# A conditioned sequence network on one core: the state-space layers' sums, D term and input projection placed at other units, and the output rows of layer 3 gathered one batch later

## The reference

```python
xn = layernorm(x) * (1 + scale) + shift          # layer 3: then xn = xn[:, perm]
x_in, z = split(xn @ W_in)                       # 512 channels each
u = silu(conv1d(x_in, 4 taps) + conv_b)
dt_r, B, C = split(u @ W_xproj)                  # 64, 16 and 16 columns
dt = softplus(dt_r @ W_dt + b_dt)
for t in range(512):                             # lax.scan over the tokens
    h = h * exp(dt[t] * A) + (dt[t] * u[t]) * B[t]    # 512 channels x 16 states
    y[t] = sum over the states of h * C[t]
y = (y + u * D) * silu(z)
out = x + gate * (y @ W_out)                     # layer 3: rows of y @ W_out permuted back first
```

## Time and profile before

| | |
|---|---|
| time of the kernel, median of 3 runs | 3458.78 us (3453.95 to 3459.62) |
| the profiled execution's own time | 3459.08 us |
| its span, first to last instruction | 3457.4 us |
| busy: PE, DVE, ACT, POOL | 78%, 74%, 62%, 50% of the span |
| layer 1, first scan to last POOL product of batch 7 | 444.42 to 1471.55 us |
| layer 3, the same | 2337.66 to 3419.28 us |

### The profile page before, as it was taken

The page is one execution under the profiler, slowest core; times in us unless marked ns, Lnnn a source line. Parts: engine busy times, 40 slices in busy tenths (PEclk is TensorE's granted clock), DMA queues, the critical chain, the costliest instruction groups (busy, mean ns, idle before and its releaser), DMA issues. The chain is left out here.

```text
span 3457.4 us, 37654 instructions
## 1 busy us (share of the span) xinstructions
PE 2700.9 (78%) x11156; PEld 1445.5 (42%) x11156; DVE 2564.7 (74%) x3375; ACT 2152.1 (62%) x3536; POOL 1716.6 (50%) x1221
## 2 busy tenths in 40 slices
PE   5787578878887887837888888847887788777885
PEld 4555244445444454522333333314444444444443
DVE  2444278898898888956777777528889888888895
ACT  0333378778778778713555555537876776768773
POOL 0000058777778778930000000016787777878785
PEclk9899689999999999967998899968999899999998
DMA  2000100111111011126444444010111101111111
GB/s 88 25 24 31 65 31 33 44 45 52 43 45 51 32 51 51 38 63 86 69 81 75 74 75 69 20 65 31 45 39 49 64 32 65 41 57 51 41 60 45
DMA packets 104195, 176.61 MB, mean 51 GB/s; under 512 B 10741, under 2 KB 91421, under 8 KB 95166
## 3 DMA queue, kind: packets, MB, share of 16 engines
q1 hardware_dynamic: 99775, 161.69, 17.6%
q0 software_dynamic: 4224, 12.59, 1.1%
HBM read 139.70 MB, written 34.14 MB: 50 GB/s over the span
## 5 line engine op out<-in xcount | busy, mean ns | idle before, releaser
L1025 POOL TENSOR_TENSOR l_h<-l_h,l_c_all 128x512 f32<-128x512 f32 x1024 | 1482.4, 1458 | 466.8 <-DVE l_h L954 438.9
L954 DVE TENSOR_TENSOR_SCAN l_h<-l_dA,l_ps_dbu 128x512 f32<-128x512 f32 x1024 | 1218.1, 1206 | 263.6 <-PE l_ps_dbu L1176 166.0
L826 ACT ACTIVATE l_dub<-l_duT,l_b_tok 128x512 f32<-128x512 f32 x1024 | 726.0, 713 | 340.4 <-PE l_ps_dbu L1176 334.6
L1176 PE MATMUL l_ps_dbu<-ident,l_dub 128*128 128x128 f32 x4096 | 643.3, 290 | 259.0 <-DVE l_h L954 176.9
L1176 PEld LDWEIGHTS l_ps_dbu<-ident,l_dub 128*128 128x128 f32 x4096 | 499.2, 148 | 685.1 <-DVE l_h L954 332.4
L840 ACT ACTIVATE l_dA<-l_dt,l_a_neg 128x512 f32<-128x512 f32 x1024 | 726.3, 713 | 0.2
L1608 ACT ACTIVATE l_probs<-l_ring 128x512 f32<-128x512 f32 x512 | 284.5, 598 | 307.4 <-PE l_ring L1732 304.6
L1163 PE MATMUL l_ps_y<-l_h,ident 128*128 128x512 f32 x768 | 430.1, 644 | 51.8 <-DVE l_h L919 49.3
L1441 DVE TENSOR_REDUCE l_q_max<-l_ring 128x1 f32<-128x512 f32 x512 | 327.9, 681 | 149.9 <-PE l_ring L1725 145.3
L984 POOL DMA_INDIRECT l_x_in<-x_dram,l_idx_x x32 | 37.3, 1167 | 739.3 <-DMA l_idx<-in_idx 733.0
L919 DVE TENSOR_TENSOR l_h<-l_h 128x512 f32<-128x512 f32 x384 | 350.0, 915 | 11.6 <-POOL l_h L1025 11.4
(11 more groups left out here) (218 smaller groups left out, 3029.4 us busy)
## 6 DMA issues: line engine op xcount, KB each, us to landing
l_c_all<-c_rows_dram SPq DMA_DIRECT2D x64, 1024.0 KB, 4.7
l_res<-x_dram SPq DMA_DIRECT2D x24, 512.0 KB, 5.6
parts_dram<-l_parts SPq DMA_DIRECT2D x48, 256.0 KB, 2.7
l_qs<-parts_dram SPq DMA_DIRECT2D x48, 256.0 KB
l_ks<-parts_dram SPq DMA_DIRECT2D x48, 256.0 KB
l_x_in<-x_dram SPq DMA_DIRECT2D x16, 512.0 KB, 4.7
x_dram<-l_res SPq DMA_DIRECT2D x16, 512.0 KB, 3.0
su_cond_w<-in_cond_w SPq DMA_DIRECT2D x1, 5120.0 KB, 15.4
```

Of the source, the lines that this page charges most:

```text
L826: return act.activation(dub[:, n % 2, t, :], duT[:, p, t, :], ACT.Copy, scale=b_tok[:, p, t, n:n + 1])
L954: dve.tensor_tensor_scan(h[:, h_slot(s), :], dA[:, s % DA_RING, :], ps_dbu[:, dbu_slot(s), :], 0.0, ALU.mult, ALU.add).then_inc(scan_ok, 1)
L1025: pool.tensor_tensor(h[:, h_slot(s), :], h[:, h_slot(s), :], c_all[:, (n // C_GROUP) % 2, n % C_GROUP, :], ALU.mult).then_inc(hc_ok, 1)
L1176: last = pe.transpose(ps_dbu[:, dbu_slot(s), t * P:(t + 1) * P], dub[:, n % 2, t, j * P:(j + 1) * P], ident[:])
```

## The change

In both layers the sums on PE are placed by channel block: blocks 0, 1, 2, 3 lie 7, 8, 10 and 7 units behind, and the earlier state of block 3 gets its product in a unit of its own (`sum_even`). Modulo 8 they stand at 2, 3, 5, 6 and 0, one each. Block 3 now completes ahead of block 2, so waits on the count of sums go through `sums_to`, and `y_gate` runs at 4, 6, 7 and 9. The D term no longer opens the accumulation and stands at units 33, 39, 57 and 60. The input projection runs in the order x0, x1, z0, x2, z1, x3, z2, z3 at units 12, 15, 17, 20, 23, 25, 28 and 31; `xn_half` is one unit earlier; the fourth block's taps stand at 28 to 31 and unit 27 has none; SiLUs, the projections behind them and softplus move by one or two units; `out_proj` stands at 47, 49, 51, 52 and `out_gate` at 50 and 54.

In layer 3, for batches 0 to 5, the gather of the output rows and its two adds move from units 56 to 63 of the next batch to units 18 to 24, 27 and 30 of the batch after that, between the gathers of x, which move to 17, 19, 21 and 23. SP's store of the result and load of the residual move with them. Batches 6 and 7 keep the old places. The loop is cut so that batch 1 stands ahead of it.

```diff
-ADD_LAG, SUM_LAG = 3, 7
+ADD_LAG = 3
+SUM_LAG = (7, 8, 10, 7)
+SUM_PLACE = (0, 1, 3, 2)
...
+X_TURN, Z_TURN = (0, 1, 3, 5), (2, 4, 6, 7)
...
 def pair_of(s):
...
+def sums_to(q):
+    return q // JB * JB + SUM_PLACE[q % JB] + 1
...
         def batches(eng, body):
...
+body(1, 1, True, True, True)
...
-    body(two * 2 + 1, 1, True, True, True)
...
-body(B - 3, (B - 3) % 2, True, True, True)
+    body(two * 2 + 3, 1, True, True, True)
...
     def body(b, p, has_post, has_prep, has_far):
-        if has_post:
+        if has_post and not gathered:
...
+        if has_post and gathered:
+            if not early(b):
+                out(b - 2)
+            res_load(b - 1)
...
-            out(b - 1)
+            if not (gathered and has_prep):
+                out(b - 1)
...
     def x_part(b, j):
-        act.wait_ge(in_mm, b * 2 * JB + 2 * j + 1)
+        act.wait_ge(in_mm, b * 2 * JB + X_TURN[j] + 1)
...
     def z_part(b, p, j):
-        act.wait_ge(in_mm, b * 2 * JB + 2 * j + 2)
+        act.wait_ge(in_mm, b * 2 * JB + Z_TURN[j] + 1)
...
     def prep_step(s, b, p):
...
-        if s in (10, 12): mod(b, (s - 10) // 2)
-        if s in (14, 18, 22, 26): x_part(b, (s - 14) // 4)
-        if s in (16, 20, 24, 28): z_part(b, p, (s - 16) // 4)
-        if s == 32: silus(b, p)
-        if s == 36: xd(b, p)
-        if s in (40, 42, 44, 46): dt_raw(b, (s - 40) // 2)
-        if s in (41, 43, 45, 47): softplus_exp(b, (s - 41) // 2)
-        if s in (42, 44, 46, 48): softplus_log(b, (s - 42) // 2)
+        if s in (9, 11): mod(b, (s - 9) // 2)
+        if s in (14, 17, 22, 27): x_part(b, (14, 17, 22, 27).index(s))
+        if s in (19, 25, 30, 32): z_part(b, p, (19, 25, 30, 32).index(s))
+        if s == 33: silus(b, p)
+        if s == 38: xd(b, p)
+        if s in (41, 43, 45, 47): dt_raw(b, (s - 41) // 2)
+        if s in (42, 44, 46, 48): softplus_exp(b, (s - 42) // 2)
+        if s in (43, 45, 47, 49): softplus_log(b, (s - 43) // 2)
...
     def y_gate(b, p, j):
-        dve.wait_ge(sum_ok, b * PAIRED + PAIRED - JB + j + 1 + CREDIT)
+        dve.wait_ge(sum_ok, b * PAIRED + sums_to(PAIRED - JB + j) + CREDIT)
...
-        if 15 <= s < 15 + JB * TAPS: tap(b, (s - 15) // TAPS, (s - 15) % TAPS)
-        if s == 37: b_copy(b, p)
-        if s in (44, 46, 48, 50): softplus_sum(b, p, (s - 44) // 2)
+        if 15 <= s < 27: tap(b, (s - 15) // TAPS, (s - 15) % TAPS)
+        if 28 <= s < 32: tap(b, JB - 1, s - 28)
+        if s == 39: b_copy(b, p)
+        if s in (45, 47, 49, 51): softplus_sum(b, p, (s - 45) // 2)
...
     def post_step(s, b, p):
...
-        if s in (4, 5, 6, 7): y_gate(b, p, s - 4)
-        if s in (49, 52): out_gate(b, p, (s - 49) // 3)
+        if s in (4, 6, 7, 9): y_gate(b, p, (0, 1, 3, 2)[(4, 6, 7, 9).index(s)])
+        if s in (50, 54): out_gate(b, p, (s - 50) // 4)
...
-                dve.wait_ge(sum_ok, b * PAIRED + pair_of(s)[0] - JB + 1 + CREDIT)
+                dve.wait_ge(sum_ok, b * PAIRED + sums_to(pair_of(s)[0] - JB) + CREDIT)
...
-                dve.wait_ge(sum_ok, b * PAIRED + pair_of(s + JB)[0] - 2 * JB + 1 + CREDIT)
+                dve.wait_ge(sum_ok, b * PAIRED + sums_to(pair_of(s + JB)[0] - 2 * JB) + CREDIT)
...
     def body(b, p, has_post, has_prep, has_far):
...
-                if s == 16: next_rows(b + 2)
-                if s in (18, 20, 22, 24): gather_x(b + 2, (s - 18) // 2)
-            if gathered and has_post:
+                if s == 15: next_rows(b + 2)
+                if s in (17, 19, 21, 23): gather_x(b + 2, (s - 17) // 2)
+            if gathered and not early(b):
+                if s in (18, 20, 22, 24): gather_y(b - 2, p, (s - 18) // 2)
+                if s in (27, 30): residual_rows(b - 2, (s - 27) // 3)
+            if gathered and has_post and not has_prep:
...
-                if not gathered and s in (51, 54): residual(b - 1, (s - 51) // 3)
+                if not gathered and s in (52, 56): residual(b - 1, (s - 52) // 4)
...
-            if has_prep and s in (44, 46, 48, 50): dt_u(b + 1, 1 - p, (s - 44) // 2)
+            if has_prep and s in (45, 47, 49, 51): dt_u(b + 1, 1 - p, (s - 45) // 2)
...
     def in_proj(b, e):
-        if e == 0:
+        turn = X_TURN[e] if e < JB else Z_TURN[e - JB]
+        if turn == 0:
...
-        elif e < JB:
-            pe.wait_ge(z_ok, b * JB + e)
+        elif turn - 1 in X_TURN:
+            pe.wait_ge(xc_ok, b * JB + X_TURN.index(turn - 1) + 1)
...
-            pe.wait_ge(xc_ok, b * JB + e - JB + 1)
+            pe.wait_ge(z_ok, b * JB + Z_TURN.index(turn - 1) + 1)
...
     def prep_step(s, b, p, after_post):
-        if first(b) and s == 10:
+        if first(b) and s == 9:
...
-        if s in (9, 11): xn_half(b, (s - 9) // 2)
-        if s in (12, 16, 20, 24): in_proj(b, (s - 12) // 4)
-        if s in (14, 18, 22, 26): z_proj(b, (s - 14) // 4)
-        if s in (34, 35): x_proj(b, p, s - 34)
-        if s == 37: b_turn(b, p)
-        if s in (39, 41, 43, 45): dt_proj(b, p, (s - 39) // 2)
+        if s in (8, 10): xn_half(b, (s - 8) // 2)
+        if s in (12, 15, 20, 25): in_proj(b, (12, 15, 20, 25).index(s))
+        if s in (17, 23, 28, 31): z_proj(b, (17, 23, 28, 31).index(s))
+        if s in (36, 37): x_proj(b, p, s - 36)
+        if s == 39: b_turn(b, p)
+        if s in (40, 42, 44, 46): dt_proj(b, p, (s - 40) // 2)
...
     def skip_term(b, p, j):
-        if first(b):
-            if j == 0:
-                pe.wait_ge(diag_ok, 1)
+        if first(b) and j == 0:
+            pe.wait_ge(diag_ok, 1)
+        pe.matmul(ps_y[:, j, :], diag_d[:, j, :], u[:, p, j, :], start=False, stop=False, skip_group_check=True)
+    def sum_even(b, s):
+        pe.wait_ge(hc_ok, b * UNITS + s + 1 + CREDIT)
+        pe.matmul(ps_y[:, DIRECT, :], ident[:], h[:, h_slot(s), :], start=(s == DIRECT), stop=False, skip_group_check=True)
+    def sum_pair(b, s):
+        n, j = s // JB, s % JB
+        q, s0 = pair_of(s)
+        if q < JB and not first(b):
+            pe.wait_ge(y_ok, b * JB - JB + SUM_PLACE[j] + 1)
+        if j == DIRECT:
+            if q < JB:
+                sum_even(b, s0)
+            pe.wait_ge(hc_ok, b * UNITS + s + 1 + CREDIT)
+            pe.matmul(ps_y[:, j, :], ident[:], h[:, h_slot(s), :], start=False, stop=(n == N - 1), skip_group_check=True).then_inc(sum_ok, 1)
...
-            pe.wait_ge(y_ok, b * JB - JB + j + 1)
-        pe.matmul(ps_y[:, j, :], diag_d[:, j, :], u[:, p, j, :], start=True, stop=False, skip_group_check=True)
-    def sum_states(b, p, s):
-        n, j = s // JB, s % JB
-        if n % 2:
-            q, s0 = pair_of(s)
-            if q < JB:
-                skip_term(b, p, j)
-            if j == DIRECT:
-                pe.wait_ge(hc_ok, b * UNITS + s + 1 + CREDIT)
-                pe.matmul(ps_y[:, j, :], ident[:], h[:, h_slot(s0), :], start=False, stop=False, skip_group_check=True)
-                pe.matmul(ps_y[:, j, :], ident[:], h[:, h_slot(s), :], start=False, stop=(n == N - 1), skip_group_check=True).then_inc(sum_ok, 1)
-            else:
-                pe.wait_ge(add_ok, b * ADDED + adds_before(q) + 1 + CREDIT)
-                pe.matmul(ps_y[:, j, :], ident[:], h[:, h_slot(s0), :], start=False, stop=(n == N - 1), skip_group_check=True).then_inc(sum_ok, 1)
+            pe.wait_ge(add_ok, b * ADDED + adds_before(q) + 1 + CREDIT)
+            pe.matmul(ps_y[:, j, :], ident[:], h[:, h_slot(s0), :], start=(q < JB), stop=(n == N - 1), skip_group_check=True).then_inc(sum_ok, 1)
+    def sums(b, at):
+        for j in range(JB):
+            s = at - SUM_LAG[j]
+            if 0 <= s < UNITS and s % (2 * JB) == JB + j:
+                sum_pair(b, s)
+        s = at - SUM_LAG[DIRECT]
+        if 2 * JB <= s < UNITS and s % (2 * JB) == DIRECT:
+            sum_even(b, s)
...
     def body(b, p, has_post, has_prep, has_far):
...
-            if s >= SUM_LAG:
-                sum_states(b, p, s - SUM_LAG)
-            elif has_post:
-                sum_states(b - 1, 1 - p, UNITS - SUM_LAG + s)
+            if has_post:
+                sums(b - 1, UNITS + s)
+            sums(b, s)
+            if s in (33, 39, 57, 60):
+                skip_term(b, p, (33, 39, 57, 60).index(s))
...
-            if has_post and s in (47, 48, 50, 51):
-                out_proj(b - 1, (47, 48, 50, 51).index(s))
+            if has_post and s in (47, 49, 51, 52):
+                out_proj(b - 1, (47, 49, 51, 52).index(s))
...
-    for s in range(UNITS - SUM_LAG, UNITS):
-        sum_states(B - 1, (B - 1) % 2, s)
+    for s in range(UNITS, UNITS + max(SUM_LAG)):
+        sums(B - 1, s)
...
```

## The result

The changed kernel takes 3462.39 us (median of 20 runs, 3453.41 to 3474.70); the kernel before, measured beside it, 3454.03 us (20 runs, 3438.55 to 3470.30). The profiled execution has a span of 3459.9 us against 3457.4 before.

A forecast was written before the change was run, and what follows sets the result against it. No engine bounds the whole kernel: PE bounds units 12 to 16, DVE 16 to 32, ACT 32 to about 48. Terms -56 - 3 + 6 - 2 - 6 = -61 us from 3458.78 give 3398 us, range 3367 to 3444.

The forecast's parts named there:

- Units 16 to 56: Middle and end of each batch: later tap and SiLU, `dt_proj` and output gate sum to +0.4 us, 6 us in all.
- the late tap: Tap at unit 31 meets a DVE add: +1.7 us, 0.5 given back, +1.2 going through ACT's SiLU in full.
- Units 12 to 15: Spreading PE's load at units 11 to 16 starts scan 15 4.0 us earlier: 14 x 4.0 = 56 us less.
- Layer 3's gathers: Layer 3: 40 us gained in the last eight units, costs at units 17 to 32 and in batch 7; sum -6 us.
- The 2 us for each add: POOL's adds at units 27 and 30 of layer 3: each costs 2 us, bounds 0 and 6.6 us.
- Rival (b): POOL starves DVE at units 27 and 30, 6.6 us for each add: 46 us more, 3444 us; chance 0.10.
- D terms at 33, 39, 57 and 60: Products moved to these units cost nothing; without cover at 57 and 60 they cost 14 x 1.7 us.
- Batch 7 and the layers' ends: Batch 7, units 12 to 16: 3 us less for two layers; one product less on the last chains: 2 us less.
- Rival (e): No change that can be measured: the stall of unit 13 moves to a later unit; chance 0.04.
- Rival (c): PE's clock at 1.2 GHz in units 12 to 16: about 4 us more a batch, 3510 us; chance 0.06.
- ACT full from 33 to 49: Sign for the profile after: ACT has no idle time from unit 33 to unit 49 of a batch.
- three named ways to be wrong: DVE taps of 4 us or more at units 28 to 31, new PE waits at 57 to 63, lower clock at 8 to 20.

The follow-up runs named there:

- both places mended: Changed kernel with `x_proj` back at units 34 and 35 and the first output projection at 48 in place of 47: 3359.85 us, ratio 0.9722 to the kernel before.

## Why the prediction was wrong

The step that failed is "Units 16 to 56", with its sum of +0.4 us a batch. That paragraph prices the late tap, `dt_proj` and the output gate, and never prices two steps that the diff moves against others: `x_proj` from 34 and 35 to 36 and 37, and the chain of `dt` by one unit under a first output projection that stays at 47. The text even had both facts at hand, "ACT's first SiLU waits for the last tap" and "everything to unit 48 hangs on ACT", but followed only ACT's own queue. It did not ask what stands ahead of a moved PE instruction in PE's order, and what that waits for. What the runs showed in place of the +0.4 us a batch are two waits of PE for ACT, at unit 36 and at unit 47, and with both taken out units 16 to 55 are 109 us shorter over the 14 batches, 7.8 us a batch.

Its terms against what the runs gave, over the 14 batches:

- **Units 12 to 15, -56 us.** Measured -56.8, with 0.56 and 0.94 us of idle time ahead of scans 13 and 14 in batch 4 of layer 1, under the 1 us named. 4.3 of the 56.8 go with the gathers (they are gone with the gathers at their old places), so 52.5 stand against the forecast. With the D terms put back 30.3 us are lost again, 2.2 a batch against the 1.7 of their products. That the turn put behind and the earlier start bring the rest was argued and not tried by itself. Right in size, and the stall that it named is gone.
- **Units 16 to 55, +6 us.** Measured +119.1, of which the gathers have 4.5. With `x_proj` and the first output projection in their mended places it is +10.0, and without the gathers +5.5. Split once more, units 16 to 47 of that kernel take 22.0 us more without the gathers (the forecast has 14 x 1.5 for tap and `dt` chain) and units 48 to 55 take 16.5 less (14 x 1.1 for the gate). So what was priced was right in size, and the two steps that were not made 109 us. That the gate is what brings the 16.5 is not shown: in the kernel before, the sums' new places alone bring 33.6 there.
- **The late tap.** The tap at unit 31 took 1.75 us and the SiLU waited for it, as written. With the preparation early again units 16 to 47 are 19.1 us shorter (1.4 a batch, against the 1.5 forecast for tap and `dt` chain) and units 48 to 55 8.8 longer; 10.3 us in all, 0.7 a batch, so not the full amount went through to the end.
- **Layer 3's gathers, -6 us.** Removed: -40 forecast, -39.0 measured in units 56 to 63. Added in units 16 to 31: 26 forecast, 4.5 measured. Batch 7: 7.3 forecast, 6.5 measured. The 2 us for each add were the mis-sized term: the two adds cost next to nothing at unit 27, which has no tap in the changed kernel, and at unit 30, where the tap behind it takes 1.75 us with or without the add; it costs 1.1 us a batch where a tap stands at unit 27. The 4.3 us at units 12 to 15 were not forecast at all. Rival (b), 6.6 us each, is ruled out. The profile after shows the long add at a batch's end in batch 7 alone (7.80 us for three). By the Trainium skill, SBUF — State Buffer, section "SBUF: two separate sides", the two engines share a port pair as a lock that is held for one whole instruction. Read as a wait for one of POOL's instructions at most, the tap's extra 1.05 us beside an add of 1.26 agrees, and the three adds of 7.80 us do not. The forecast by that rule, 8 us lower, was nearer for this term.
- **D terms at 33, 39, 57 and 60, nothing.** Units 56 to 63 of layer 1 went from 93.1 to 91.8 us over seven batches, and putting the D terms back changes them by 0.1 and units 32 to 39 by 2.4 over all 14. Right for the changed kernel; in the kernel before, the sums' placement with its D terms cost 10.8 us at units 36 to 39 and 5.8 at units 56 to 63 of layer 1, which was not taken apart.
- **Batch 7 and the layers' ends, -5 us.** Batch 7 of layer 1 is 2.6 us shorter; that of layer 3 4.1 longer, with the 6.5 of its gathers in it, so 5.0 less without them against the 3 forecast. The last `y_gate` starts 1.4 and 1.2 us sooner behind the last scan, against 0.9 forecast for each end.
- **Units 0 to 11.** Not forecast: -10.9 us, and -13.1 with the sums' placement alone. A gain that the prediction left out.
- **Rival (e), no change.** Its time, 3459 us, was the nearest to the one measured, but not by its mechanism: the stall of unit 13 went away, and the new ones come from other steps.
- **Rival (c), the clock.** The granted clock was 1.00 in the windows of units 12 to 19 of every batch but one. In units 8 to 11 it lay between 0.80 and 1.00 in most batches, much as before; in batch 3 of layer 3 it was 0.50 there, and behind it the first turn took 2.31 us, scan 13 waited 2.00, and units 12 to 15 took 8.86 us in place of the 7.40 of the batches beside it. So the mechanism exists, for 1.5 us in one batch of 14; it did not decide.

Of the signs named for the profile after, those of unit 12 (but for batch 3 of layer 3), of the tap, of PE's wait for `og` (1.2 us at the longest), of the last eight units in layer 3 (13.4 us, 93.7 over seven batches) and of the long adds came true. Units 16 to 31 of layer 3, batches 2 to 5, did not take 5 us more for the gathers but 0.7 (39.7 us against 39.0 with the gathers at their old places). ACT full from 33 to 49 did not: 6.68 of 10.18 us at unit 36, because it waited for the very projection. That sign was the one to read. Of the three named ways to be wrong, only the lower clock at units 8 to 20 occurred, in that one batch.

Put together: -61, with -28 for the gathers (-39.0 + 4.5 + 6.5) in place of -6 and -11 for units 0 to 11, gives -94. The kernel with both places mended has a span 99.2 us below that of the kernel before. That the two lie close owes something to the two terms put in after the fact; with them the forecast of the change's other parts holds, and the change as made spends the gain on two steps.

What stays open: why the new places of the sums bring 33.6 us at units 48 to 55 was seen but not taken apart, and in the kernel before `x_proj` at 36 was not tried with ACT's copy moved along. Why 6.5 us come back at units 44 to 47 when `x_proj` alone is moved was not followed either.

## What to carry to other kernels

An in-order engine makes every instruction inherit the waits of those ahead of it, so when a step moves, list what stands between its old and its new place on its own queue and what each of these waits for, and then who waits for the step's result on the others. The best place for short independent work is behind its input and ahead of the next instruction that waits for a busy engine: there even a product of 3.47 us cost next to nothing, and two units later the same step cost some 5 us a batch. When a chain of steps is shifted, shift every user of the buffer that it passes through, and in a diff of unit numbers look for the one number that did not change.
